# Q's first block from exact codes, and the attention loop's side work placed anew

## The reference

```
x = x + attention(layernorm(x))      # q, k, v, o weights are 4-bit codes with a scale per 128 inputs
x = x + xattn(layernorm(x), ctx)     # both operands fake-quantised, then one matmul
x = x + layernorm(x) @ binarised(weight)
```

```
w = (codes - 8) * scales[input // 128, column]
q = rope(h @ wq);  k = rope(h @ wk);  v = h @ wv
out = softmax(q @ k.T / sqrt(128) + mask) @ v
return out @ wo
```

## Time and profile before

| | us |
|---|---|
| median of 3 runs | 1104.35 |
| lowest and highest | 1102.6, 1105.29 |
| span of the profiled execution | 1104.9 |
| TensorE busy in it | 1056.7 |
| VectorE busy | 934.1 |
| ScalarE busy | 690.9 |
| GpSimd busy | 689.6 |

### The profile page before, as it was taken

How to read it: one execution, slowest core, us unless ns; L and a number is a source line. 1 busy time by engine, 2 the same in 40 slices (tenths; PEclk the granted TensorE clock), 3 DMA queues, 4 the chain that set the end, 5 groups by cost and what they waited for, 6 DMA issues and landing times.

```text
span 1104.9 us, 18938 instructions
## 1 busy us (share of the span) xinstructions
PE 1056.7 (96%) x5448; PEld 513.8 (47%) x5448; DVE 934.1 (85%) x1755; ACT 690.9 (63%) x1502; POOL 689.6 (62%) x770
## 2 busy tenths in 40 slices
PE   3898999899999999999999999999999999989998
PEld 2443444444544444444444444544544544444443
DVE  7977897799888888888888889999999998888873
ACT  4455665766777777777777776666666666463320
POOL 2457546877767766776777677777878777332200
PEclk9999999999999999999999999999999999999999
DMA  9344231767678667657766765777777675432453
GB/s 350 123 135 132 67 101 44 150 149 170 142 155 160 145 147 159 159 134 154 163 148 141 159 160 130 148 155 162 151 150 171 142 128 119 108 117 53 101 103 79
DMA packets 301204, 153.65 MB, mean 139 GB/s; under 512 B 249264, under 2 KB 261808, under 8 KB 301136
## 3 DMA queue, kind: packets, MB, share of 16 engines
q1 hardware_dynamic: 293360, 139.46, 55.3%
q10 hardware_dynamic: 7776, 13.37, 4.4%
HBM read 89.07 MB, written 4.19 MB: 84 GB/s over the span
## 4 chain that ended last, share of the span: by engine, by line
PE 78%; DVE 8%; ACT 5%; POOL 3%; issue 3%; ACTq 1%; DMA 1%; SPq 1%; DVEq 0%; POOLq 0%
PE side_ps L699 10%; PE side_ps L856 9%; PE side_ps L701 9%; PE side_ps L700 9%; PE proj_ps L876 8%; PE out_ps L876 8%; PE proj_ps L1027 4%; PE score_ps L839 3%; PE score_ps L841 2%; PE score_ps L840 2%; PE proj_ps L1032 2%; PE score_ps L998 2%; PE out_ps L719 2%; PE score_ps L719 2%; PE proj_ps L699 2%
## 5 line engine op out<-in xcount | busy, mean ns | idle before, releaser
L1534 POOL TENSOR_TENSOR w_b<-prob,w_b 128x896 f16<-128x896 f32 (+2 forms) x192 | 188.9, 998 | 30.6 <-ACT w_b L1222 30.0
L699 PE MATMUL side_ps<-hT,w_a 128*128 128x512 f16 x504 | 191.1, 379 | 1.5 <-DVE rot L1895 1.5
L701 PE MATMUL side_ps<-hT,w_a 128*128 128x512 f16 x504 | 191.0, 379 | 0.0
L700 PE MATMUL side_ps<-hT,w_a 128*128 128x512 f16 x504 | 191.0, 379 | 0.0
L1990 DVE SCALAR_TENSOR_TENSOR x_acc<-proj_ps,o_now,x_acc 128x1024 f32<-128x1024 f32 x120 | 153.6, 1280 | 37.8 <-PE proj_ps L876 37.8
L1527 POOL TENSOR_SCALAR prob<-prob,row_inv 128x512 f32<-128x512 f32 (+3 forms) x256 | 170.7, 681 | 22.6 <-DVE row_inv L2063 16.9
L1195 ACT ACTIVATE prob<-score_ps,neg_max 128x512 f32<-128x512 f32 (+3 forms) x256 | 132.9, 521 | 47.4 <-DVE neg_max L1966 38.6
L1541 POOL TENSOR_TENSOR q_sb<-rot,q_sb 128x512 f16<-128x512 f32 x64 | 75.0, 1172 | 139.8 <-ACT q_sb L1187 139.8
L1990 DVE SCALAR_TENSOR_TENSOR x_acc<-out_ps,o_now,x_acc 128x1024 f32<-128x1024 f32 x120 | 152.7, 1272 | 0.0
L876 PE MATMUL proj_ps<-work,w_b 128*128 128x512 f16 x496 | 127.3, 379 | 1.9 <-DVE x_acc L1990 1.1
L876 PE MATMUL out_ps<-work,w_b 128*128 128x512 f16 x496 | 127.3, 379 | 1.3 <-DVE x_acc L1990 1.2
(11 more groups left out here) (238 smaller groups left out, 2102.5 us busy)
## 6 DMA issues: line engine op xcount, KB each, us to landing
stage_c<-in_codes_dram SPq DMA_DIRECT2D x80, 256.0 KB, 2.9
stage_o<-in_codes_dram SPq DMA_DIRECT2D x64, 256.0 KB, 3.9
stage_s<-in_scales_dram SPq DMA_DIRECT2D x64, 256.0 KB, 3.8
ctx_raw<-in_ctx_dram ACTq DMA_DIRECT2D x32, 256.0 KB, 3.2
work<-w_b SPq DMA_TRANSPOSE x261, 3.0
x_acc<-in_x_dram SPq DMA_DIRECT2D x8, 512.0 KB, 8.5
k_sb<-in_codes_dram SPq DMA_DIRECT2D x16, 256.0 KB, 6.4
v_sb<-in_scales_dram SPq DMA_DIRECT2D x16, 256.0 KB, 7.3
```

What stands on the lines that cost most here:

```text
L699: pe.matmul(o, stat(0), mov(0), start=first, stop=False)
L700: pe.matmul(o, stat(0), mov(1), start=False, stop=False)
L701: return pe.matmul(o, stat(1), mov(0), start=False, stop=last)
L1534: ins = pool.tensor_tensor(prob16[:, 1, to:to + w], prob[:, at:at + w], prob16[:, 0, to:to + w], ALU.subtract)
```

## The change

Q's first input block (kb = 0) of every slot from 4 on is made from bare codes: ScalarE writes `codes - 8` for those 128 columns of the piece, and TensorE makes two matmuls into pv_ps (`q_exact`). ScalarE evicts that bank with Q's scale for the block into an SBUF tile (`q_base`), and VectorE adds the bank of the other seven blocks to it (`q_join`). The swap reads this tile; GpSimd makes the cosine (`q_turn`) behind the sine, both now early in slot p + 1; VectorE's sum comes after the third maxima, ScalarE's upper half after the third exponentials, GpSimd's lower half after the first two norms. The attention rest moves from the end of VectorE's slot to behind the first maxima of the next. O's codes are converted ahead of the probabilities' upper half, from one stage, and loaded by SyncE after the feed-forward transfers. The second stage holds Q's scales at first and the new tile later. The scales of Q's first block stand as a ninth column in O's table.

```diff
+EXACT = P
+EARLY = 2
+Q_LEAD = 3
-        o_now = sb("o_now", [P, 2, CB], F32)
+        o_now = sb("o_now", [P, 2, CB + 1], F32)
+        k_scale = prob[:, D:D + KB * NKV].rearrange("p (c r) -> p c r", c=KB // 2)
+        q_scale_rows = stage_o[:, 1, 0:NH * KB].bitcast(F32)
+        q_sum_in = stage_o[:, 1, :].bitcast(F32)
+        def by_parts(p):
+            return not (known(p) and p < FIRST_PIECES)
...
 sync
+            sp.dma_start(q_scale_rows, q_scales).then_inc(q_scale_landed, 16)
-                if not (known(p) and p + 1 >= N_SLOTS):
-                    if not (known(p) and p == 0):
-                        sp.wait_ge(q_ready, p + 1)
-                        sp.wait_ge(o_codes_done, p)
-                    load_o(o_index(*after), (i + 1) % 2)
+            def next_o(g, i):
+                p = g * SLOTS + i
+                after = (g, i + 1) if i + 1 < SLOTS else (g + 1, 0)
+                sp.wait_ge(o_codes_done, p + 1)
+                load_o(o_index(*after), (i + 1) % 2)
...
+                    if not (known(p) and p + 1 >= N_SLOTS):
+                        next_o(g, i)
                     turn(p)
...
 tensor
+            def q_exact(g, i):
+                h = i // B
+                p = g * SLOTS + i
+                pe.wait_ge(piece_done, g * SLOTS + (2 * h + 2))
+                pe.wait_ge(ao_ready, p - 3)
+                for l in range(2):
+                    mm = pe.matmul(pv_ps, w_a[:, 0, h % RING * KB * P:(h % RING * KB + 1) * P],
+                                   hT[:, l, 0, i % B * S:(i % B + 1) * S], start=l == 0, stop=l == 1)
+                mm.then_inc(q_exact_done, 1)
...
-                if kbs[0] == 0:
+                first = 1 if by_parts(p) else 0
+                if kbs[0] == first:
...
-                        pe.wait_ge(q_summed, p)
+                        pe.wait_ge(q_joined, p - FIRST_PIECES)
...
 weigh
+                if not (known(p) and (p == 0 or p >= N_SLOTS - FIRST_PIECES + 1)):
+                    pe.wait_ge(q_based, p)
...
 slot
-                if has_ahead:
+                parts = by_parts(p + Q_AHEAD)
+                if has_ahead and parts:
+                    q_exact(*ahead)
+                elif has_ahead:
                     q_part(*ahead, range(0, 1))
+                if has_ahead and parts:
+                    q_part(*ahead, range(1, EARLY))
                 scores(p, i, g, 2)
                 if has_ahead:
-                    q_part(*ahead, range(1, 3))
+                    q_part(*ahead, range(EARLY if parts else 1, 3))
...
 scalar
+                if exact:
+                    act.activation(w[:, 0, col:col + exact], stage_c[:, r, 0:exact], ACT.Copy, bias=-CODE_ZERO)
+                act.activation(w[:, 0, col + exact:col + PIECE], stage_s[:, r, exact:PIECE], ACT.Copy, scale=up)\
...
-                swap(q_bank(p), q_swapped)
+                if by_parts(p):
+                    act.wait_ge(q_joined, p - FIRST_PIECES + 1)
+                swap(q_sum_in if by_parts(p) else q_bank(p), q_swapped)
+            def q_base(g, i):
+                p = g * SLOTS + i
+                act.wait_ge(q_exact_done, p - FIRST_PIECES + 1)
+                if not (known(p) and p == FIRST_PIECES):
+                    act.wait_ge(q_cosed, p)
+                if known(p) and p < Q_LEAD * B:
+                    act.wait_ge(q_scale_ready, 1)
+                else:
+                    act.wait_ge(o_now_ready, g * RF + (i // B - (Q_LEAD - 1)))
+                act.activation(q_sum_in, pv_ps, ACT.Copy, scale=o_now[:, (i // B + 1) % 2, CB:CB + 1])\
+                    .then_inc(q_based, 1)
...
-                if has_next:
+                if has_next and not by_parts(p + 1):
                     q_hi(p + 1)
                 exps(p, i, 1)
+                if has_ahead and by_parts(p + Q_AHEAD):
+                    q_base(*((g, i + Q_AHEAD) if i < SLOTS - Q_AHEAD else (g + 1, i + Q_AHEAD - SLOTS)))
...
                 exps(p, i, 2)
+                if has_next and by_parts(p + 1):
+                    q_hi(p + 1)
                 if has_piece:
                     q_cut(p, i)
...
+                o_cut(p, i)
                 prob_split(p, 0)
...
                 prob_split(p, 1)
-                o_cut(p, i)
...
 gpsimd
+            def q_turn(p):
+                pool.wait_ge(q_joined, p - FIRST_PIECES + 1)
+                pool.wait_ge(q_ready, p)
+                pool.tensor_tensor(rot[:, :], q_sum_in, cos_t[:, :], ALU.mult).then_inc(q_cosed, 1)
...
+                    if not (known(p) and p >= N_SLOTS - 1) and by_parts(p + 1):
+                        sine(q_swapped, p + 1, q_sined)
+                        q_turn(p + 1)
...
                     norm(2).then_inc(norm_done, 1)
+                    if not (known(p) and p >= N_SLOTS - 1) and by_parts(p + 1):
+                        q_lo(p + 1)
...
 vector
+            def q_join(p):
+                dve.wait_ge(q_done, p + 1)
+                dve.wait_ge(q_based, p - FIRST_PIECES + 1)
+                dve.tensor_tensor(q_sum_in, q_bank(p), q_sum_in, ALU.add).then_inc(q_joined, 1)
...
+                dve.wait_ge(q_scale_landed, 16)
+                rows = q_scale_rows.rearrange("p (h k) -> p h k", k=KB)
+                dve.tensor_scalar(o_table[:, 0:NH - Q_LEAD, CB], rows[:, Q_LEAD:NH, 0], Q_UP, None, ALU.mult)
...
 slot
-                if i or known(p):
+                first = not (i or known(p))
+                if not first:
+                    maxima(p, i, 0)
+                if first:
+                    dve.wait_ge(q_ready, p + 1)
+                if has_prev and p_ge2:
+                    ao_rest(p - 2, (i - 2) % SLOTS)
+                if first:
                     maxima(p, i, 0)
...
-                if has_next:
+                if has_next and not by_parts(p + 1):
                     q_sum(p + 1)
...
                 maxima(p, i, 2)
+                if has_next and by_parts(p + 1):
+                    q_sum(p + 1)
...
-                if has_piece:
-                    piece_lo(n, i % 2, q_region(i), Q_UP)
                 if has_o:
                     o_add(p, i, 1)
+                if has_piece:
+                    piece_lo(n, i % 2, q_region(i), Q_UP, (EXACT, 0)[i % B])
...
+                if has_ahead and by_parts(p + Q_AHEAD):
+                    q_join(p + Q_AHEAD)
                 if has_o:
                     o_add(p, i, 2)
...
-                if has_ahead:
+                if has_ahead and not by_parts(p + Q_AHEAD):
                     q_cos(p + Q_AHEAD)
-                if has_prev:
-                    ao_rest(p - 1, (i - 1) % SLOTS)
```

More of the change, by code:

```diff
@@ L1099, in next_roots, with piece @@
                 act.activation(root[:, 1, c0:c0 + k], root[:, 0, c0:c0 + k], ACT.Sqrt).then_inc(root_ready, 1)
-            def piece(n, r, region, up, free):
+            def piece(n, r, region, up, free, exact=0):
                 w, col = region
@@ L1213, in q_cut @@
                 free = (q_done, p + (RING - i % B))
-                piece(p + FIRST_PIECES, i % 2, q_region(i), Q_UP, free)
+                piece(p + FIRST_PIECES, i % 2, q_region(i), Q_UP, free, (EXACT, 0)[i % B])
             def prob_split(p, part):
@@ L1641, in body @@
                     prob_rest(p, 0)
-                    if not (known(p) and p >= N_SLOTS - Q_AHEAD):
+                    if not by_parts(p + Q_AHEAD):
                         sine(q_swapped, p + Q_AHEAD, q_sined)
@@ L2017, in slot @@
                 n = p + FIRST_PIECES
+                p_ge2 = not (known(p) and p < 2)
                 if known(p) and p == N_SLOTS - 1:
@@ L2047, in slot @@
                     wf_difference(0)
-                if has_next:
+                if has_next and not by_parts(p + 1):
                     q_sum(p + 1)
-                if not (i or known(p)):
-                    maxima(p, i, 0)
                 if has_o and not (known(p) and p == O_LAG):
```

49 lines of the change are left out of this document (29 added, 20 removed).

## The result

The changed kernel takes 1109.89 us (median of 6 runs, 1107.14 to 1110.29) against 1104.14 us of the kernel before on the same chips (1102.6 to 1105.6): ratio 1.0045, 95% interval [1.0034, 1.0057]. It is slower by half a per cent where 1.6% faster was forecast.

What follows compares the result with a forecast made beforehand. TensorE's instruction stream was taken as the bound. From 1104.35 us, -13.0 (matmuls) - 10.2 (stalls) + 3.2 (copy) + 1.0 (slot 3) + 0.3 + 1.2 (rest's lateness) = -17.5 gave 1086.9 us, range 1079.5 to 1097.

Steps and rivals of the forecast that it cites:

- (1): TensorE, Q's first block: two matmuls for three save 0.216 us in each of 60 slots, 13.0 us.
- (7): First and last slots: slot 3's 1 us stall stays; the end costs nothing, bounds -1 and +2.
- Step (5): New waits on GpSimd, ScalarE and VectorE's join: cost nothing, with 0.8 us of cover.
- the GpSimd ring: Chain of GpSimd and ScalarE instructions, 10.9 us round, deciding only from 11.68 us on, after 0.8 us of stretch.
- Rival B: GpSimd ring stretched by slower operations to 12.5 us a slot: +25 us, 1129 us; chance 0.07.
- step (2): VectorE's maxima before the attention rest, O's codes moved on ScalarE: stalls go, up to 10.2 us gained.
- step (3): VectorE's small copy of O's scales, held by GpSimd's product: 0.2 us in 16 odd slots, 3.2 us lost.
- The prediction's 1 us for slot 3: Slot 3, among the first slots: its stall of 1 us stays because the attention rest is late; 1.0 us charged.

Runs made afterwards that it cites:

- E7: Kernel before the change, with eight already-met waits more a slot in ScalarE's loop: 1109.62 us, ratio 1.0038.
- E2: Changed kernel with ScalarE's swap of Q's halves moved behind the second split of the probabilities, from slot 2 on: 1112.67 us, ratio 1.0059.
- E5: Changed kernel with O's scale copy behind the attention remainder, ScalarE's implied waits out, swap behind split in weight-work and first eight slots: 1089.2 us, ratio 0.9862.
- E9: Kernel before the change, with 24 already-met waits more a slot in ScalarE's loop: 1109.91 us, ratio 1.0044.
- E4: Changed kernel without ScalarE waits that other waits imply, in slots whose Q is made in parts: 1104.12 us, ratio 0.9991.
- E1: Changed kernel with VectorE's copy of O's scales moved behind the first maxima and the attention remainder in odd slots: 1106.5 us, ratio 1.001.
- E6: E5 plus the attention remainder ahead of the first-half maxima on VectorE in odd slots: 1085.07 us, ratio 0.9820.
- E10: E6 with ScalarE's implied waits put back: 1085.3 us, ratio 0.9823.
- E3: Changed kernel with GpSimd's addition for the feed-forward weights moved behind Q's turn of the next slot: 1104.65 us, ratio 0.9989.

## Why the prediction was wrong

**Steps (1) and (7).** Two products for three gave what was forecast: the clean slot is 11.67 us for 11.90, and TensorE's busy time fell by 11.8 us for 13.0. The end was late by 1.5 us, within the bound of +2. 0.8 us of it is a wait for a transfer ahead of L1065, 2.4 us for 1.6, which every changed version has; what makes it late wasn't tried. The other 0.7 comes and goes with the execution: E7, which has the kernel before in this stage, took 140.8 us there, E2 and E5 140.4, and 20 to 40 us behind the last weighing the granted clock is 0.83 in E7 and in the change, 0.91 in E2, E5 and the kernel before. That slots 61 to 64 took what they took before is luck: in the profiled execution of the kernel before, the weighing of slot 62 ran at the lower clock, 3.07 us for 1.79, and in E7 to E9 the same code took 36.4, 35.9 and 36.0 us. Against those the change lost 1.1 to 1.6 us there, and the versions with the copy moved have it back (36.3 to 36.6).

**Step (5), the one that failed most.** It says: "The join waits for Q's last matmul at 9.4, ends 10.1, the swap 11.3", and "Cost nothing; cover 0.8 us on the GpSimd ring (below)." Q's last matmul was in time: in the slot shown, which starts at 820.52, it ends at 831.13, 10.6 in the slot with a stall of 1.3 ahead of it. But the join isn't started by it. It stands near the end of VectorE's row and begins 1.6 us later, at 832.77, with VectorE never idle since the sum. The swap therefore falls into the next slot, from 0.6 to 1.9 of it, and what stands behind it moves along: the second split, GpSimd's second remainder (at 3.1, where 1.3 was written), the sine, the cosine (done at 7.3, where 5.6 was written), and VectorE's sum, from which its row leads to the next join. I had priced this as a ring of GpSimd and ScalarE, 10.9 us; the one that decides also takes 4.9 us of VectorE's row, from sum to join, and is 12.31 us long. It cost 9.7 us in the slots with weight work: that is what E2, and E5 again, take back there by moving one instruction. Rival B had the right kind of mechanism, but left VectorE's row out of the ring and needed its operations stretched by 1.2 us in all before the kernel became slower. The ring as it is needed no stretch at all. What I should have written for each new wait is not only when the waiting instruction is due, but which instruction *behind* it on the same engine is the next link.

**No step at all: ScalarE's code.** New instructions were priced by their time on the engine, and the waits by what they wait for. That they are also instructions had no term. The three turns of the loop cost 3.7 us in their own slots; E4 takes them away and the loop is 4.3 us shorter, and E7 puts them into a kernel that never had them. The entry is another matter: slot 9 takes 12.49 us, but 12.03 in E1 with the longer code and 12.33 in E4 with the shorter, so it isn't the code's. In the version of E6 nearly all of this price is hidden again (E10), so it isn't a constant of the gap but depends on what else is late. The Trainium skill names this, in "Runtime: NRT & Kernel Launch", section "Instruction fetch mechanics": code is fetched ahead in sequence, and a taken branch whose target lies outside a small window of blocks stops the engine for the fetch. I had not weighed that rule. The traces agree with it: a gap behind the pass's last instruction, ordinary slots of the old length inside the body even with 24 waits a slot, and a step between 6 and 32 instructions.

**Steps (2) and (3): the sizes.** The maxima ahead of the attention's remainder did end the stall of the third score block: in the window of the loop TensorE's weight loads waited for the exponential 3 times, 4.7 us, for 31 times and 16.2 us, and the wait on VectorE's rotated sum is gone. But step (2) let the maxima begin at 0.85 in the slot and the remainder end "at 2.15 + 0.05" where the output block is due at 2.16. In E1, without the copy in the way, the maxima begin at 0.96 and the remainder ends at 2.27, and from its end to the matmul are 0.24 us, not 0.05 (602.51 + 0.69 = 603.20, 603.44; the slot starts at 600.93). The two terms make the 0.35 us. The odd slots lost 0.39 us each in the loop and 0.2 with weight work, 8 us, where 4.4 were charged. In step (3) the copy is held for 1.33 us and ends with GpSimd's product, which agrees with the rule that the prediction cites there from the Trainium skill, "SBUF — State Buffer", section "Who interferes with whom". The times of step (3), maxima at 1.0 and the remainder's end at 2.3, came true to 0.01 us. But the price of the copy was overrated in the loop, since without it the maxima would have waited for the scores until 0.96: taking it away makes an odd slot 0.04 us shorter (E1), 0.6 us in all for 3.2. What was charged to the copy belonged to the order. The order itself was the wrong one in odd slots: E6, which takes the remainder first, gains 4 us over E5, 2.1 with weight work, 1.7 in the loop, and 0.6 in the first slots.

**The first slots.** The prediction's 1 us for slot 3 was what the slot took beyond a clean one, and the slot has four output matmuls less, 0.86 us; so the kernel before had 2.0 us of stalls in it (13.06 less 11.03). They became one of 2.38 us, with a copy of 1.72 us held by GpSimd ahead of it, and the slot 13.19: 0.5 us more than forecast. 13.19 is its length in E2 to E4; E1 shortens it to 12.64, E5 to 11.87, E6 to 11.20. In the profiled execution of the change itself the same slot took 14.87 us, as TensorE's granted clock fell soon after the stall:
```profile
219.00:224.00 5.00, 4.93 (x17) 2.20 (x18) 3.42 (x10) 2.73 (x11) 3.93 (x6) 0.66 0.69 127
```
Its matmuls of 512 columns there start 0.43 us apart for 0.216, the 1.2 GHz level. E2 to E4 have the same stall and no such stretch, so 1.7 us of the table's 85.4 are of this one execution.

**The sum.** 1108.5 measured less 1087.4 forecast for the span is 21.1 us: 9.7 for the ring and 1.5 for the order in the stage with weight work, 4.3 for the code (by E4) and 2.5 for the order in the loop (beyond the 3.8 charged there), 2.6 in the first slots, of which 1.7 are the stretch at the lower clock, and 1.5 at the end, less 0.9 at the start and 0.1 in slots 61 to 64. Split this way by reading, the terms are rough; what the experiments show is that E6, which moves three instructions and leaves out waits, reaches 1085.07 where 1086.9 was forecast. It comes there by other edits than the prediction had in mind, so it shows that the steps were worth what was forecast, not that the forecast was right. The gain of the change was real and was taken back by the order in which it was put.

## What to carry to other kernels

When a new wait is put on an engine, follow the instruction behind it, and the one that this releases on the next engine, until the chain returns to where it began; its length against the slot is the price, and no engine's busy share shows it. An instruction moved within its own queue can then be worth more than a matmul saved: one swap behind one split gave 9.7 us in 21 slots, where the matmul gives 4.5. Look at every stage before moving it: in the loop the same move cost 14 us (E2). For a loop, count the instructions and the waits that its body holds, compare the packets of the engine's instruction queue, and look at the first instruction after each end of a pass. When a stage of one execution is compared with that of another, look at its granted clock first.

## What the runs showed of the hardware

- The cost of a longer loop body is a step. ScalarE's queue moved 36 packets with 6 to 8 instructions a pass more and 52 with some 30 or 95 more, and the gap at the end of a pass was 1.7 us in place of 0.2 with either. In the changed kernel it was 1.2 to 2.1, in E10 1.0 to 1.1.
- Waits that are already met cost next to nothing in the loop of the kernel before: 24 a slot left its ordinary slots at 12.06 and 12.17 us, but for one in eight of 12.47. On a chain without slack they count: three fewer a slot took 0.19 us off every second slot with weight work (E4).
- A copy of 9 elements a row on VectorE ended with the GpSimd instruction it had started in: 1.33 us in the slot shown (604.27 and 604.24), 1.72 in slot 3. In the kernel before such a copy, of 8, took 0.16 us at its least.
- VectorE's sum of two SBUF tiles took 0.69 us in the loop (E2), 0.83 with weight work and 1.11 in the mean where GpSimd's addition ran beside it (E3).
- A stall of 2.38 us ahead of a matmul was followed in one execution by a stretch at the 1.2 GHz level, and in three others of like kernels by none.
